# A graph layer with two routed-expert blocks: routing work moved, table lookups shared, the last sums added in place

## The chip, the cores and the metric

One Trainium2 chip, one of its cores. The metric is device microseconds (us) of one execution. Engines in the rows: PE is TensorE's matmul, PEld its weight load, DVE VectorE, ACT ScalarE, POOL GpSimd, SP SyncE, which issues transfers. A letter q behind an engine's name (PEldq, SPq, POOLq) means its sequencer.

## The reference

x has 1250 rows (nodes) of 512 float32, with 40000 edges. Two layers, each a graph part plus a linear-attention mix, and then experts:

```python
xn = layernorm(x)
x = x + L0_gnn(xn, src, dst, ...) + L0_mix(xn[None], ...)[0]
x = x + L0_ffn(layernorm(x)[None], ...)[0]
xn = layernorm(x)
x = x + L1_gnn(xn, edge_index, ...) + L1_mix(xn[None], ...)[0]
x = x + L1_ffn(layernorm(x)[None], ...)[0]

# the experts of either layer, with their own activation:
p = softmax(x @ gate_w)                       # 16 experts
w, idx = top_k(p)                             # 4 in layer 0, 2 in layer 1; weights normalised
y = sum over e of w_e * (act(x @ w1[e] + b1[e]) @ w2[e] + b2[e])    # only for the rows that chose e
y = y + shared experts of every row           # 2 in layer 0 (halved), 1 in layer 1
```

Layer 0 has 256 hidden columns and Gelu. Layer 1 has 384 pairs of gate and up columns with a clamped SwiGLU.

## The kernel before

The program is a row of stages. Each is a block in which every engine has its own instruction list; a stage begins on an engine when all have left the one before. Rows of x stand in ten tiles of 125. The residual is `st.res3`.

**Setup** (L136) loads edges, x in two halves, three small parameter rows, then the mix weights. VectorE works on the edges, waits for the turned parameters (L277, copy L278) and then takes the row moments of x.

**Norm** (`stage_layernorm`, L301): ScalarE's square root (L340), VectorE's reciprocal and scaling, TensorE turns the ten tiles (L334), ScalarE places them (L343). SyncE has nothing here.

**Experts, front** (`stage_front`, L1045). SyncE loads gate, biases, shared weights, b2, writes the normed rows to the DRAM table, and loads the first experts. TensorE makes the logits of three chunks of nodes (500, 500, 250) (L1202) and turns them (L1207). VectorE picks the experts (L1421 to L1452, `mask_ready`) and makes the combine weights (L1468, `comb_ready`). Meanwhile TensorE makes the shared up products in units (one block of hidden columns of one chunk, L1227): 12 units in layer 0, 9 in layer 1. After unit COUNT_AFTER (4 in layer 0, 2 in layer 1) it counts the marks (L1232, L1233, `counted`), and VectorE runs `find_places` (L1325 to L1393), a chain of small instructions that gives each row its slot in a tile of 128 slots and each tile its expert. In layer 1 VectorE's clips and products of the shared SwiGLU (`clip`, `mix`, L1482 to L1494) stand behind `find_places` in its list; ScalarE takes a unit out of PSUM (L1302, L1304) into a ring of four, and TensorE has two pairs of banks for it. After all units TensorE turns the combine weights (L1241), ScalarE places them (L1322), and then the ten shared down tiles follow (L1265, L1267), with `find_rows` (L1251) before the fourth. VectorE adds each to the residual (L1529), and SyncE writes it to the DRAM tensor `token_sums` (L1160).

**Experts, routed** (`stage_routed`, L1906). The number of tiles and each tile's expert are known only on the chip, so the loops are made of registers. There are 48 tiles in layer 0 and 28 in layer 1. For tile g TensorE makes `raise_up(g)` (L2057), then `turn_hidden(g-1)` (L2066), `turn(g+1)` (L2047) and `bring_down(g-1)` (L2075). A matrix product is two passes of an instruction. Before each raise_up and each bring_down its sequencer reads the tile's expert and ring slot from SBUF (`expert_of` L1951, `ring_of` L1954). VectorE adds the bias (L2149) and places the rows (L2142, L2143), ScalarE places the turned hidden rows (L2103), applies Gelu or the sigmoid (L2111, L2108) and weighs the result (L2117).

GpSimd, in one list per tile (L2000): a copy of the row numbers (L1981), the gather of the rows of tile g+4 (L1988), a wait until all adds of earlier experts have landed (L2009), and the add of tile g's result into `token_sums` (L1996). ScalarE's weighing waits for that copy (L2115).

SyncE loads expert e into a ring of three when expert e-3 has been brought down (L962, `load_expert` L992). At the end of layer 0 it reads `token_sums` back; at the end of layer 1 it copies them to the output (L1974) and waits.

## Time and profile before

| | us |
|---|---|
| runs of before, median of 3 (lowest, highest) | 2489.71 (2486.22, 2492.75) |
| the profiled execution, its own time | 2487.18 |
| its span | 2485.1 |
| PE busy | 2205.3 (89%) |
| DVE busy | 1001.1 (40%) |
| ACT busy | 513.2 (21%) |
| POOL busy | 286.9 (12%) |

The profiled execution's own time is 2.1 us over its span and 2.5 us under the median of the runs. A busy TensorE is not one at its peak. What a stage is worth is read from its own stretch of time.

### The profile page before, as it was taken

Reading aid. Unit: us, or ns where it says so; the run is one execution under the profiler, and the core shown is the slowest. Engines: PE = TensorE matmul, PEld = TensorE weight load, DVE = VectorE, ACT = ScalarE, POOL = GpSimd, SP = SyncE. Lnnn points to the kernel's source line nnn. Section 1 sums busy time; section 2 is a strip of 40 time slices with the busy share of each in tenths; the row PEclk is TensorE's granted clock in tenths of the full one; section 3 lists DMA queues with packets and bytes.
Section 4 is the critical chain, followed back from the end, with each engine's and each line's share of the span. In section 5 each row is a group of like instructions: output and inputs, shape, how many; then the busy total and the mean of one; then the engine's idle time right before and its main releaser. Section 6 shows DMA issues by size and latency. Waiting matters only on the chain. (4 is left out here: it accounts for less than half of the span.)

```text
span 2485.1 us, 26904 instructions
## 1 busy us (share of the span) xinstructions
PE 2205.3 (89%) x7344; PEld 1258.0 (51%) x7345; DVE 1001.1 (40%) x2721; ACT 513.2 (21%) x900; POOL 286.9 (12%) x317
## 2 busy tenths in 40 slices
PE   5998979999989988884998899989899898799996
PEld 3444435444454454442543388834488644445553
DVE  7967874302035321222043464311355223634443
ACT  1112221110113022222110254211243112202111
POOL 1200000000000144441200000000000100013332
PEclk9999999999999999997999999989999899899998
DMA  4003000000004267666001000020000103048684
GB/s 119 1 0 112 1 1 17 0 17 0 0 1 135 64 146 167 151 151 151 1 0 59 0 1 1 1 92 0 1 1 1 39 0 127 12 152 274 194 259 115
DMA packets 77265, 159.34 MB, mean 64 GB/s; under 512 B 9133, under 2 KB 20440, under 8 KB 77116
## 3 DMA queue, kind: packets, MB, share of 16 engines
q1 hardware_dynamic: 59516, 115.62, 14.1%
q0 software_dynamic: 17664, 42.64, 8.7%
q8 instruction: 47, 0.77, 0.1%
q14 instruction: 38, 0.31, 0.0%
HBM read 122.06 MB, written 38.74 MB: 65 GB/s over the span
## 5 line engine op out<-in xcount | busy, mean ns | idle before, releaser
L1812 PE MATMUL bank<-arena 125*125 125x257 f32 x1600 | 355.7, 383 | 4.7 <-DVE arena L1731 4.7
L1812 PEld LDWEIGHTS bank<-arena 125*125 125x125 f32 x1600 | 302.2, 189 | 60.4 <-DVE arena L1731 6.3
L2057 PE MATMUL bank<-arena 128*128 x832 | 250.4, 451 | 25.5 <-issue 14.0
L937 PE MATMUL bank<-arena 125*128 125x500 f32 (+1 forms) x720 | 253.0, 512 | 2.3 <-ACT arena L957 2.3
L2057 PEld LDWEIGHTS bank<-arena 128*128 128x128 f32 x832 | 156.6, 194 | 140.8 <-issue 81.4
L1627 PE MATMUL bank<-arena 128*125 128x512 f32 x480 | 211.1, 600 | 8.7 <-DMA arena<-in_L_gnn_W 8.7
L465 PE MATMUL bank<-arena 128*125 128x512 f32 x480 | 213.9, 595 | 2.2 <-PEq L307 1.1
L2075 PE MATMUL bank<-arena 128*128 x360 | 175.3, 616 | 37.7 <-ACT arena L2103 29.8
L937 PEld LDWEIGHTS bank<-arena 125*128 125x128 f32 x720 | 135.6, 189 | 120.0 <-issue 110.1
L2149 DVE TENSOR_TENSOR arena<-bank,arena 128x384 f32<-128x384 f32 (+1 forms) x104 | 51.6, 497 | 307.7 <-PE bank L2057 306.6
L1790 ACT ACTIVATE arena<-arena 125x625 f32<-125x625 f32 x160 | 134.5, 901 | 102.4 <-DVE arena L1731 102.2
L1627 PEld LDWEIGHTS bank<-arena 128*125 128x125 f32 x480 | 90.6, 191 | 122.8 <-issue 113.2
L465 PEld LDWEIGHTS bank<-arena 128*125 128x125 f32 x480 | 87.3, 188 | 102.3 <-issue 101.0
L1731 DVE SCALAR_TENSOR_TENSOR arena<-arena 125x625 f32<-125x625 f32 x160 | 132.4, 864 | 15.9 <-ACT arena L1790 15.9
L1996 POOL DMA_INDIRECT token_sums<-arena x76 | 121.3, 1596 | 147.8 <-DMA token_sums<-arena 97.9
L1663 DVE CUSTOM_DVE_ANT_0 arena<-arena 125x256 f32<-125x256 f32 x160 | 58.5, 421 | 184.9 <-ACT arena L1650 169.2
L756 PE MATMUL bank<-arena 125*125 125x500 bf16 x432 | 112.9, 389 | 19.8 <-DVE arena L731 18.9
L874 DVE TENSOR_TENSOR arena<-bank,arena 128x500 f32<-128x500 f32 (+1 forms) x36 | 21.3, 592 | 264.4 <-PE bank L937 264.4
L731 DVE TENSOR_SCALAR arena<-arena 125x500 bf16<-125x500 f16 x432 | 117.8, 345 | 23.5 <-PE bank L756 22.8
L919 PE MATMUL bank<-arena 128*125 128x512 f32 x240 | 110.1, 622 | 14.6 <-DVE arena L853 9.4
L2075 PEld LDWEIGHTS bank<-arena 128*128 128x128 f32 x360 | 62.3, 189 | 105.2 <-issue 105.2
L1988 POOL DMA_INDIRECT arena<-token_rows,arena x76 | 80.3, 1056 | 171.7 <-DVE arena L2143 143.5
(324 smaller groups left out, 2178.7 us busy)
## 6 DMA issues: line engine op xcount, KB each, us to landing
arena<-in_L_ffn_expert_w SPq DMA_DIRECT2D x16, 1536.0 KB
arena<-in_L_ffn_re_w SPq DMA_DIRECT2D x32, 512.0 KB, 6.4
arena<-in_L_ffn_expert_w SPq DMA_DIRECT2D x16, 768.0 KB, 10.6
arena<-in_L_mix_Wqkv SPq DMA_DIRECT2D x6, 1024.0 KB, 16.4
arena<-in_L_ffn_expert_b SPq DMA_DIRECT2D x16, 384.0 KB
token_rows<-arena SPq DMA_DIRECT2D x2, 2500.0 KB
token_sums<-arena SPq DMA_DIRECT2D x20, 250.0 KB
arena<-in_L_gnn_W SPq DMA_DIRECT2D x1, 4096.0 KB, 12.8
```

The lines of the kernel that those rows point to most:

```text
L465: last = pe.matmul(st.bank[n % 4][0:TS, :], st.turned[:, k, t * TS:(t + 1) * TS], w3[:, k, j * D:(j + 1) * D], start=(k == 0), stop=(k == ...
L731: last = dve.tensor_scalar(marks[:, u, :], st.iota16[:, 0:WIN * NT], float(w * WIN * NT), keys[:, u:u + 1], ALU.add, ALU.is_equal)
L756: last = pe.matmul(bank, stays[:, u, :], marks[:, u, :], start=False, stop=False, skip_group_check=True)
L919: last = pe.matmul(st.bank[s % 4][0:TS, :], X[:, k, s * TS:(s + 1) * TS], w[:, k, :], start=(k == 0), stop=(k == KT - 1))
L937: last = pe.matmul(st.bank[4 + n % 4][:, 0:cn], h[:, s, f * P:(f + 1) * P], st.counts[:, s, c0:c0 + cn], start=(s == 0), stop=(s == NT - 1))
L1627: last = pe.matmul(st.bank[n % 4][0:TS, :], x, w[:, k, half * 512:(half + 1) * 512], start=(k == 0), stop=(k == K - 1))
L1731: dve.scalar_tensor_tensor(out=prob[:, u % 2, s, :], in0=excess[:, n % EXCESS, :], scalar=by_one[:, s, head:head + 1], in1=st.counts16[:, ...
L1790: act.activation(excess[:, n % EXCESS, :], row[:, head, d0:d0 + HALF], ACT.Relu, scale=by_fifth[:, s, head:head + 1], bias=minus_one[:, s, ...
L1812: return pe.matmul(st.bank[n % OUTS][0:TS, 0:ONCOL], prob[:, u % 2, s, j * TS:(j + 1) * TS], st.slots[:, head + 1, s, :], start=(s == 0), ...
L1996: pool.indirect_dma_start(out=sums, out_offset=bass.IndirectOffsetOnAxis(ap=own_row[b][:, 0:1].bitcast(mybir.dt.uint32), axis=0), in_=y[b] ...
L2057: last = pe.matmul(st.bank[UP[b][h]][:, 0:WP], xt[b][:, k, :], rt.ring[:, bass.ds(r, 1), k * W + h * WP:k * W + (h + 1) * WP].rearrange("p ...
L2075: last = pe.matmul(st.bank[DOWN[b]], ht[b][:, f, :], rt.ring[:, bass.ds(r, 1), W2_AT + f * D:W2_AT + (f + 1) * D].rearrange("p a n -> p (a ...
```

## The change

It does eight things.

- Setup: the copy of the turned parameters stands behind the row moments.
- A square root on one throw-away value (`fetch_root`) is put where ScalarE is free: in setup, at the end of the linear stage, and at the end of layer 0's routed stage.
- The gate weights, gate bias, activation scalars and first shared bias are loaded in the norm before the experts, on its SyncE, no longer at the front's start. The other loads of the front keep their order.
- Layer 1 counts behind the first unit, no longer behind the third.
- The combine weights are turned behind the third unit from the end, amid the up products, into banks 6, 7 and 0. Layer 1's down tiles have three banks, no longer four.
- In the routed loop TensorE reads a tile's expert and slot once, between the first and the later products of a bring_down, keeps them in registers, and turns the hidden rows of tile g-1 in the middle of raise_up(g). All lookups for tiles 0 and 1 and the tile count stand before the first raise_up.
- Layer 1's shared result is written to the output itself, and GpSimd adds to it there, with a bound that drops rows past 1249. The copy at the end goes.
- For that the row numbers are one lower.

```diff
@@ stage_setup
-            dve.memset(st.eps, EPS)
+            dve.memset(st.eps, EPS).then_inc(eps_set, 1)
...
-            dve.wait_ge(par_turned, 1)
-            dve.tensor_copy(st.par, st.bank[4][:, 0:3 * LK].rearrange("p (w x) -> p w x", w=3))
             for h, tiles in enumerate(HALVES):
                 dve.wait_ge(x_loaded[h], 32)
                 row_moments(dve, st, range(*tiles), summed)
+            dve.wait_ge(par_turned, 1)
+            dve.tensor_copy(st.par, st.bank[4][:, 0:3 * LK].rearrange("p (w x) -> p w x", w=3))
+        @block.scalar
+        def _(act):
+            act.wait_ge(eps_set, 1)
+            fetch_root(act, st)
@@ new
+def fetch_root(act, st):
+    act.activation(st.any_root, st.eps, ACT.Sqrt)
@@ stage_layernorm
+        if load is not None:
+            block.sync(load)
@@ stage_front
-    COUNT_AFTER = 2 if SW else 4
-    DOWN = [4, 5, 6, 7]
+    COUNT_AFTER = 0 if SW else 4
+    COMBINE_AFTER = NU - 3
+    COMBINE = [6, 7, 0]
+    DOWN = [4, 6, 7] if SW else [4, 5, 6, 7]
...
-            pe.wait_ge(comb_ready, 1)
-            pe.wait_ge(shared_set, 1)
-            pe.wait_ge(up_taken, TAKES * NU)
-            for t in range(NT):
-                c, at = t // 4, (t % 4) * TS
-                last = pe.transpose(st.bank[1 + c][0:total, at:at + TS], comb[:, t, :], st.ident[0:TS, 0:TS])
-            last.then_inc(comb_turned, 1)
+                if m == COMBINE_AFTER:
+                    pe.wait_ge(comb_ready, 1)
+                    pe.wait_ge(shared_set, 1)
+                    pe.wait_ge(counts_used, 1)
+                    for t in range(NT):
+                        c, at = t // 4, (t % 4) * TS
+                        last = pe.transpose(st.bank[COMBINE[c]][0:total, at:at + TS], comb[:, t, :], st.ident[0:TS, 0:TS])
+                    last.then_inc(comb_turned, 1)
...
@@ stage_routed, SyncE and GpSimd
-            else:
-                sp.dma_start(out, sums[1:NODES + 1, :]).then_inc(sums_read[0], 16)
-                sp.wait_ge(sums_read[0], 16)
...
-                    in_=y[b], in_offset=None, compute_op=ALU.add).then_inc(landed[b], 16)
+                    in_=y[b], in_offset=None, compute_op=ALU.add, **bounds).then_inc(landed[b], 16)
@@ stage_routed, TensorE
+                steps = [(h, k) for h in range(PARTS) for k in range(KT)]
+                for n, (h, k) in enumerate(steps):
+                    if n == len(steps) // 2:
+                        between()
...
-            def bring_down(g, b):
-                e, r = expert_of(pe, g), ring_of(pe, g)
+            def bring_down(g, b, r, e, between):
...
+                    if f == 0:
+                        between()
...
-            raise_up(0, 0)
-            more = more_pairs(pe)
-            with pe.Fori(0, more) as i:
-                for b in (1, 0):
-                    g = i * 2 + (2 - b)
-                    raise_up(g, b)
-                    turn_hidden(g - 1, 1 - b)
-                    turn(g + 1, 1 - b, i * 16 + 32)
-                    bring_down(g - 1, 1 - b)
+                first = place_of(0)
+                pe.reg_mov(slot_even, first[1])
+                keep_odd(place_of(1))
+                more = more_pairs(pe)
+                raise_up(0, 0, *first, nothing)
+                with pe.Fori(0, more) as i:
+                    g = i * 2 + 1
+                    odd = kept(expert_odd, NE - 1), kept(slot_odd, R - 1)
+                    raise_up(g, 1, *odd, lambda: turn_hidden(g - 1, 0))
+                    turn(g + 1, 0, i * 16 + 32)
+                    even = []
+                    bring_down(g - 1, 0, kept(slot_even, R - 1), odd[0], lambda: even.extend(place_of(g + 1)))
+                    h = i * 2 + 2
+                    raise_up(h, 0, *even, lambda: turn_hidden(h - 1, 1))
+                    turn(h + 1, 1, i * 16 + 32)
+                    pe.reg_mov(slot_even, even[1])
+                    bring_down(h - 1, 1, odd[1], even[0], lambda: keep_odd(place_of(h + 1)))
```

## Rows read from the trace of the kernel before

**Rows 1.** Busy time by stretch: length, PE, PEld, DVE, ACT, POOL, clock, DMA share, GB/s

```profile
853.00:1140.00 287.00, 227.47 (x864) 138.80 (x864) 56.48 (x144) 69.31 (x144) 136.68 (x148) 0.98 0.65 145
2200.00:2474.00 274.00, 250.44 (x812) 138.37 (x812) 119.95 (x280) 49.88 (x84) 84.19 (x88) 0.97 0.71 208
```

**Rows 2.** Setup's parameter copy (timeline: start, length, engine, line); square root's table loads (ns)

```profile
18.59 0.20 DVE L278 COPY arena<-bank 128x36 f32<-128x36 f32 x1 [2.35 <-PE bank L298]
...
L340 ACT ACT_TABLE_LOAD  x3: 1283/1283/1283, 25.7 to 2061.2; - x3
```

**Rows 3.** TensorE at the start of layer 0's front, layer 1's front, and the mix

```profile
750.81 0.42 PE L1196 MATMUL bank<-arena 16*128 16x16 f32 x4 [2.85 <-DMA arena<-in_L_ffn_gate_w]
...
L1202 PE MATMUL bank<-arena 128*16 128x500 f32 (+1 forms) x24 | 11.5, 647 | 4.8 <-DMA arena<-in_L_ffn_gate_w 4.8
...
1169.97 0.30 PE L448 MATMUL bank<-arena 128*128 128x128 f32 x1 [1.14 <-PEq L307]
```

**Rows 4.** Timeline of layer 0's front, TensorE between up and down products

```profile
798.07 1.23 PE L1241 MATMUL bank<-arena 125*18 125x125 f32 x10 [0.70 <-ACTq L1313]
...
800.89 5.20 PE L1265 MATMUL bank<-arena 128*125 128x512 f32 x8 [1.60 <-ACT arena L1322]
```

**Rows 5.** Timeline of layer 1's front

```profile
2087.46 20.40 PE L1227 MATMUL bank<-arena 128*128 128x500 f32 x48
2094.34 0.25 DVE L1452 TENSOR_SCALAR arena<-arena 125x160 f32<-125x160 f32 x1
2095.74 0.33 DVE L1468 TENSOR_TENSOR arena<-arena 125x160 f32<-125x160 f32 x1
2108.54 0.07 DVE L1336 MEMSET arena<- 125x16 f32 x1 [12.48 <-PE bank L1233]
2132.90 0.54 DVE L1482 TENSOR_SCALAR arena<-arena 128x500 f32<-128x500 f32 x1
2137.70 12.48 PE L1227 MATMUL bank<-arena 128*128 128x250 f32 x48 [9.18 <-ACT arena L1304]
2157.04 5.45 PE L1265 MATMUL bank<-arena 128*125 128x512 f32 x6 [4.63 <-ACT arena L1322]
```

**Rows 6.** Timeline of one tile of layer 1's routed loop

```profile
2240.41 5.32 PE L2057 MATMUL bank<-arena 128*128 x16
...
2245.90 0.60 PE L2047 MATMUL bank<-arena 128*128 128x128 f32 x4
...
2246.84 2.84 PE L2075 MATMUL bank<-arena 128*128 x6 [0.34 <-ACT arena L2103]
...
2249.52 5.36 PE L2057 MATMUL bank<-arena 128*128 x16
...
2249.86 0.62 DVE L2168 SCALAR_TENSOR_TENSOR arena<-arena 128x384 f32<-128x384 f32 x1
```

**Rows 7.** Layer 0's routed loop: timeline of one tile, and the sequencer's loads (ns, minimum/median/maximum)

```profile
1103.82 1.99 PE L2057 MATMUL bank<-arena 128*128 x8 [0.48 <-issue]
...
1106.70 1.98 PE L2075 MATMUL bank<-arena 128*128 x4 [0.23 <-ACT arena L2103]
...
1109.24 1.99 PE L2057 MATMUL bank<-arena 128*128 x8 [0.56 <-issue]
...
L1951 PEldq TENSOR_LOAD <-arena x94: 297/306/1211, 862.6 to 1129.7; - x94
```

**Rows 8.** Layer 0's routed loop: adds of one expert's tiles, and a load of weights

```profile
927.92 1.60 POOL L1996 DMA_INDIRECT token_sums<-arena  x1 [6.19 <-DMA token_sums<-arena]
933.09 0.37 SPq L998 DMA_DIRECT2D arena<-in_L_ffn_re_w  x1
935.74 1.60 POOL L1996 DMA_INDIRECT token_sums<-arena  x1 [0.30 <-issue]
944.12 1.60 POOL L1996 DMA_INDIRECT token_sums<-arena  x1 [4.43 <-DMA token_sums<-arena]
```

**Rows 9.** The line L1974, copy to the output: issue to landing

```profile
DMA to landing us min/median/max: 9.7/9.7/9.7
```

More of the change, by code:

```diff
@@ L1002, in load_expert, with front_inputs, load, stage_experts @@
     sp.dma_start(w2, ins[kind.w2][e].rearrange("(f p) n -> p f n", p=P)).then_inc(rt.w2_loaded, 16)
-def stage_experts(nc, st, ar, kind, ins, kept, out=None, load=None):
+def front_inputs(nc, ar, kind, ins):
+    fi, total = State(), NE + kind.shared
+    fi.brow_w = 2 * P if kind.swiglu else P
+    fi.gw = ar.take(KT * NE).rearrange("p (k e) -> p k e", k=KT)
+    fi.gw_rows = None if kind.gate_b else ar.take(D, NE)
+    fi.gb = ar.take(NE, TS) if kind.gate_b else None
+    fi.act5 = ar.take(total * 5) if kind.swiglu else None
+    fi.b1_rows = ar.take(fi.brow_w, kind.shared * (kind.w1_cols // fi.brow_w))
+    fi.gw_loaded, fi.gb_loaded, fi.act_loaded, fi.b_loaded = (
+        nc.alloc_semaphore(name=f"{what}_loaded_{kind.top}") for what in ("gate", "gate_bias", "act", "first_bias"))
+    def load(sp):
+        if kind.gate_b:
+            sp.dma_start(fi.gw, ins[kind.gate_w].rearrange("(k p) e -> p k e", p=P)).then_inc(fi.gw_loaded, 16)
+            sp.dma_start(fi.act5[:, 0:NE * 5].rearrange("p (o x) -> p o x", o=1),
+                         ins[kind.act].rearrange("e a -> (e a)").unsqueeze(0).unsqueeze(0)
+                         .to_broadcast([P, 1, NE * 5])).then_inc(fi.act_loaded, 16)
+            sp.dma_start(fi.act5[:, NE * 5:],
+                         ins[kind.sact].unsqueeze(0).to_broadcast([P, 5])).then_inc(fi.act_loaded, 16)
+            sp.dma_start(fi.gb, ins[kind.gate_b].unsqueeze(0).to_broadcast([TS, NE])).then_inc(fi.gb_loaded, 16)
+            first_bias = ins[kind.sb1].rearrange("(f n) -> f n", n=fi.brow_w)
+        else:
+            sp.dma_start(fi.gw_rows, ins[kind.gate_w]).then_inc(fi.gw_loaded, 16)
+            first_bias = ins[kind.sb1].rearrange("e (f n) -> (e f) n", n=fi.brow_w)
+        sp.dma_start(fi.b1_rows, first_bias).then_inc(fi.b_loaded, 16)
+    fi.load = load
+    return fi
+def stage_experts(nc, st, ar, kind, ins, kept, fi, out=None, load=None):
     total = NE + kind.shared
@@ L1956, in stage_routed @@
         sums = rt.sums
+        bounds = {} if out is None else dict(bounds_check=NODES - 1, oob_is_err=False)
         @block.sync
@@ L2082, in _, with kept, keep_odd @@
             turn(1, 1, 16)
-            raise_up(0, 0)
-            more = more_pairs(pe)
-            with pe.Fori(0, more) as i:
-                for b in (1, 0):
-                    g = i * 2 + (2 - b)
-                    raise_up(g, b)
-                    turn_hidden(g - 1, 1 - b)
-                    turn(g + 1, 1 - b, i * 16 + 32)
-                    bring_down(g - 1, 1 - b)
-            g = more * 2 + 1
-            raise_up(g, 1)
-            turn_hidden(g - 1, 0)
-            bring_down(g - 1, 0)
-            turn_hidden(g, 1)
-            bring_down(g, 1)
+            with ExitStack() as regs:
+                reg = lambda name: regs.enter_context(pe.register(f"{name}_{kind.top}"))
+                slot_even, expert_odd, slot_odd = reg("slot_even"), reg("expert_odd"), reg("slot_odd")
+                def kept(reg, top):
+                    return nc.s_assert_within(pe.snap(reg), 0, top)
+                def keep_odd(place):
+                    pe.reg_mov(expert_odd, place[0])
+                    pe.reg_mov(slot_odd, place[1])
+                first = place_of(0)
[15 more added lines that the diff above has]
+                    bring_down(h - 1, 1, odd[1], even[0], lambda: keep_odd(place_of(h + 1)))
+                g = more * 2 + 1
+                odd = kept(expert_odd, NE - 1), kept(slot_odd, R - 1)
+                raise_up(g, 1, *odd, lambda: turn_hidden(g - 1, 0))
+                bring_down(g - 1, 0, kept(slot_even, R - 1), odd[0], nothing)
+                turn_hidden(g, 1)
+                bring_down(g, 1, odd[1], odd[0], nothing)
         @block.scalar
@@ L2134, in _ @@
             weigh(g, 1)
+            if out is None:
+                fetch_root(act, st)
         @block.vector
@@ L2212, in build @@
         st.blockmask = held.take(P)
-        st.eps, st.eps6 = held.take(1), held.take(1)
+        st.eps, st.eps6, st.any_root = held.take(1), held.take(1), held.take(1)
         st.inv = held.take(2, TS)
```

79 lines of the change are left out of this document (35 added, 44 removed).

## The prediction

> **What bounds the kernel now.** I first read the busy times by stretch. In both routed loops TensorE is busiest, 227 of 287 us in layer 0 and 250 of 274 us in layer 1, at 0.98 and 0.97 of its clock; GpSimd has 137 us in the first and 84 in the second [rows 1]. So layer 1's loop is TensorE's. Layer 0's is open: TensorE idles 60 us there. Then I read the timelines of the places that the change touches: what TensorE waits for and for how long. A wait counts only where TensorE, or the chain that feeds it, is late; the rest of the span (graph, mix, attention) is untouched, and I cost it at nothing.
>
> **Setup and norms.** VectorE waits 2.35 us for the parameters before the row moments [rows 2]. Moved behind them, the copy still costs its 0.2 us. The parameters are issued behind x on the same queue, so x should have landed by then: 2.15 us gained; bounds 0 (x is what is late) and 2.35. The square root's table is loaded three times, 1.283 us each, on the path of the norm [rows 2]. The new calls put load and root where ScalarE waits for others: 3 x 1.28 = 3.85 us. The Trainium skill ("ScalarE: Activation LUTs", What ACT_TABLE_LOAD costs) adds 1.38 us of drain to each switch, 4.1 us more by its figure; no row here shows a drain, and the sum goes without.
>
> **Gate inputs in the norm.** TensorE waits 2.85 us in layer 0 and 4.8 in layer 1 for the gate weights; a stage begun without a load costs it 1.14 us [rows 3]. The most to gain is 1.7 and 3.7, the least I expect 1.0 and 3.0, if the stage's end costs more here: I take 4.6 for both, near the middle. Loading in the norm costs nothing: SyncE is idle there, and the issues lie beside seven us of scaling and turning. If that cover went, five issues would cost some 2 us.
>
> **Layer 0's front.** Between up and down products TensorE idles 0.70 + 1.60 us, with ten turns of 1.2 us between, and begins the down products slowly: eight passes take 5.20 us [rows 4], where six of the same width take 2.84 at the high clock [rows 6], so eight take 3.7. The turns amid the units cost the same 1.2; the waits and the slow start go: 2.3 + 1.5 = 3.8 us, at least 2.3. The weights are long ready, and the three copies on ScalarE lie beside two units.
>
> **Layer 1's front.** This is the largest part. Today [rows 5]: three units take 20.3 us, so six with the counts end at 2128.5. TensorE then idles 9.18 us until ScalarE has taken unit 4, because the ring waits for VectorE, which is in `find_places` from 2108.54 to 2132.90, 24.4 us. The last three units take 12.48 us in place of 10.2 (half clock at first), the turns and their waits reach to 2157.04, and six down passes take 5.45 us in place of 2.84.
>
> After: the mask is ready at 2094.6, unit 0 ends at 2094.2, so the count waits 0.4 us. `find_places` begins behind the combine weights, 2096.1, and ends at 2120.5. Unit 6 today starts 4.8 us after its end (2137.70 - 2132.90); that is now 2125.3, before TensorE has finished unit 5 at 2128.9. The stall is gone. Three units of 3.4 and 1.1 of turns end at 2140.2, and down begins at 2140.3: 16.7 us earlier, and 2.6 more for the full clock, 19.3. VectorE needs under 24.1 us from the end of `find_places` to its last product (2132.90 to 2157.04, when down began), so it is done by 2144.7, and only the ninth down tile needs the last ones. The fewer down banks cost nothing: VectorE's add is due three tiles later. Lower bound 16, if the ring holds TensorE by one unit.
>
> **Layer 1's routed loop.** A tile takes 9.11 us. The turns begin at 2245.90, four of 0.107 end at 2246.33, down begins at 2246.84: 0.51 us waiting for the placed hidden rows [rows 6]. Turned amid the up products, the rows have 2.6 us of products over them, and the copy is hidden. The hidden values are ready 0.96 us into the next up product (2250.48 against 2249.52), the new turn stands 2.6 in; with the period half a us shorter 0.7 us of slack remains. The lookups within bring_down are issued some 2 us ahead and have a product of 0.86 over them, so they cost nothing. 26 x 0.51 = 13.3 us gained, 0.3 at the end. Lost: all lookups before the first up product, which had two, 2.2 us by the pace of [rows 7]; 0.9 us at tile 0, whose hidden rows arrive after the midpoint of tile 1; and 1 us where the loop catches up with a weight load. Net 9.5; bounds 2 (the slack is not there) and 13.
>
> **Layer 0's routed loop.** A tile of TensorE's work is 8 x 0.214 + 6 x 0.107 + 4 x 0.43 = 4.1 us, yet 5.42 pass. From the first down product to the next up product 2.54 us pass where 1.72 are work: the lookups, two loads of 0.306 us in the median and up to 1.21 at the worst [rows 7]. Hidden placing costs another 0.4. After the change there is one pair of lookups with only 0.86 us of product and 0.44 of lead over it, so about 0.5 us stays inside bring_down: period 4.75 where TensorE binds. By the Trainium skill ("DMA: Bandwidth & Descriptors", Latency and other measured facts) such a load takes about 600 ns at least; the rows show half of that, and by its figure 0.6 us more would stay per tile.
>
> But TensorE seldom binds here. An expert's adds start at 927.92 and 935.74, two of 3.9 us each, and the next expert's first add waits until 944.12 for the last to land, 8.4 us [rows 8]: 16.2 us for three tiles, 5.4 each, whatever TensorE does. The wait is long because the next weights are loaded at 933.09, when the expert has been brought down, just ahead of that add. The lookups inside the down products end them 1.0 us later, and the load with them. I take this as 2 us lost over the ten such experts, between 8 gained and 10 lost. Six tiles at the end and three at the start meet no load; at 4.75 in place of 5.42 they gain 6.0. The lookups ahead of the first up product cost 2.2, and the end gains 0.4. Net 2.2 us gained; bounds -10 and 25.
>
> **The output.** The copy takes 9.7 us from issue to landing [rows 9], after the last add has landed, and the add must land in either kernel: 9.8 us with the wait before it. The bound on the rows is unknown in its price. GpSimd's own work per tile is 3.9 us of 9.1 [rows 6, 8], so it has over 4 us of cover, but the last add has none: 0 to 2 us, I take 0. Writing the ten shared tiles to the output costs what writing them to the scratch tensor does.
>
> **The sum.** 2.15 + 3.85 + 4.6 + 3.8 + 19.3 + 9.5 + 2.2 + 9.8 = 55.2 us. From the execution's own 2487.2 that gives 2432. Against the median of 2489.7 it is 2.3% less. What a measurement of this kernel can tell from no change is about 0.3%, 7.5 us.
>
> **Rivals.** (a) *Layer 0's loop follows TensorE after all.* For it: TensorE idles 60 us in 287. Against it: the adds' chain. All 48 tiles at 4.75 in place of 5.42 gain 32 us, less 2.2 for the lookups at the start: 28 us more than my 2.2, so 2404. (b) *The midpoint turn waits.* VectorE reads registers too; if the hidden rows come after the midpoint, TensorE now stalls with half a product still to do, and what it stood behind before was useful work. For it: only 0.7 us of slack, and a late load in layer 0's lookups. Layer 1's loop then gains 2 in place of 9.5 and layer 0's loses 8: 2432 + 7.5 + 10 = 2449. (c) *The bounded add costs more on GpSimd.* This is the mechanism for slower. GpSimd issues one in 1.6 us and has 8.6 - 3.9 = 4.7 us of room per tile. From 6.3 us per issue it sets the pace of layer 1's 28 tiles, and to eat 55 us an issue must take 1.6 + 4.7 + 2.0 = 8.3 us; at 9 it is 2432 + 28 x 2.7 = 2508. For it: no row shows a bounded one. Against it: the list of rows is the same, and a bound is a comparison. (d) *The front does not gain*, as TensorE waits elsewhere for `find_places`: the turns now wait for `counts_used`. That is ready 5.4 us into it, 2101.5, 30 us before the turns, so I give it nothing.
>
> **How the numbers follow.** Forecast 0.60; (a) 0.13; (b) 0.23, a part of which is its half-way cases; (c) 0.02; the rest 0.02, around no change. The predicted time is the forecast's, 2432. Its own bounds (layer 0's loop -10 to 25, layer 1's 2 to 13, front 16, tables) give 2412 to 2448. Eight times in ten should also take in most of (b) and half of (a): 2406 to 2452. Faster by over 0.3% 0.97, within 0.01, slower 0.02.
>
> **What would show it.** Right: no table load at the norm's root; TensorE's first product 1.1 to 1.8 us after the norm; no idle time of several us in layer 1's up products, down products there at full clock, about 39 us for ten; a tile of layer 1's loop at 8.6 us with no wait for L2103; adds of layer 0's experts still two of 3.9 and one of over 8 us; nothing after the last add. Wrong: TensorE waiting in the middle of an up product (b); layer 0's tiles under 5 us on average (a); GpSimd's add over 1.6 us (c). If the landings grow to 9 or 10 us for every expert, my 2 us for the later loads are too few.

## The result, and the profile after

| us | before | after |
|---|---|---|
| median of the runs (lowest, highest) | 2490.36 of 4 (2486.22, 2492.75) | 2422.99 of 4 (2420.39, 2426.32) |
| the profiled execution, its own time | 2487.18 | 2420.39 |
| its span | 2485.1 | 2417.9 |
| PE busy | 2205.3 (89%) | 2183.7 (90%) |
| POOL busy | 286.9 (12%) | 287.1 (12%) |

After over before is 0.9732, 95% interval 0.9713 to 0.9751: 67.4 us less. The forecast was 2432, 55.2 us less, with 2406 to 2452 as its range. The direction and the likeliest case were right. 12 us more were gained than the sum has, and that is the net of errors of both signs.

The two profiles show where. Each row below takes one instruction that both kernels have and gives its start in both; the difference is what has been gained by then, and the step from row to row is what that stretch gained.

| until the start of | before | after | so far | this stretch | forecast for it |
|---|---|---|---|---|---|
| the first norm's first turn | 28.36 | 24.70 | 3.66 | 3.66 | 3.43 (copy, one table load) |
| layer 0's logits | 751.55 | 746.79 | 4.76 | 1.10 | gate inputs, with layer 1's: 4.6 |
| its first shared up product | 762.99 | 756.53 | 6.46 | 1.70 | 0 |
| its first down tile's bias product | 806.02 | 795.36 | 10.66 | 4.20 | 3.8 |
| its last routed add | 1137.11 | 1119.17 | 17.94 | 7.28 | 2.2 |
| the reciprocal in the last norm | 2062.85 | 2041.50 | 21.35 | 3.41 | 2.57 (two table loads) |
| layer 1's logits | 2074.65 | 2049.87 | 24.78 | 3.43 | in the 4.6 above |
| its first shared up product | 2087.46 | 2059.75 | 27.71 | 2.93 | 0 |
| its first down tile's bias product | 2162.43 | 2114.98 | 47.45 | 19.74 | 19.3 |
| its last routed add | 2468.89 | 2407.07 | 61.82 | 14.37 | 9.5 |
| the end of the span | 2485.1 | 2417.9 | 67.2 | 5.4 | 9.8 |

Four stretches are off by more than 2 us: the logits of both layers (gate inputs: 9.2 for 4.6), layer 0's loop (+5.1), layer 1's loop (+4.9) and the output (-4.4).

The busy time by stretch, columns as in [rows 1], the same two loops:

```profile
842.50:1124.50 282.00, 225.89 (x864) 131.32 (x864) 56.51 (x144) 70.44 (x146) 137.12 (x148) 0.98 0.67 148
2153.00:2412.00 259.00, 242.40 (x812) 136.78 (x812) 120.09 (x280) 47.04 (x84) 83.83 (x88) 0.97 0.70 212
```

TensorE now idles 17 of 259 us in layer 1's loop, 24 of 274 before; in layer 0's it still idles 56 of 282.

**The gate and the logits.** Timeline of TensorE at the start of both fronts, in the kernel after:

```profile
746.79 8.57 PE L1235 MATMUL bank<-arena 128*16 128x500 f32 x24 [0.32 <-DVE arena L1447]
...
2049.87 8.55 PE L1235 MATMUL bank<-arena 128*16 128x500 f32 x24 [1.13 <-PEq L318]
```

and, in the kernel before, the line that answers to the first, with the busy times (columns as in [rows 1]; the clock is the third number from the end) of the first four and a half us of either layer's logits. The prediction used neither:

```profile
751.55 10.26 PE L1202 MATMUL bank<-arena 128*16 128x500 f32 x24 [0.32 <-DVE arena L1410]
```

```profile
751.50:756.00 4.50, 4.45 (x7) 0.91 (x8) 0.00 (x0) 0.00 (x0) 0.00 (x0) 0.64 1.00 330
2074.60:2079.00 4.40, 4.35 (x6) 0.88 (x7) 0.58 (x3) 1.84 (x3) 0.00 (x0) 0.50 0.76 233
```

The waits of 2.85 and 4.81 us [rows 3] are 1.13 now, as forecast. But the 24 passes behind them also went from 10.26 to 8.57 us in layer 0, and from 11.5 [rows 3] to 8.55 in layer 1. Before, they began at a granted clock of 0.64 and 0.50, the lower of TensorE's two levels (1.2 of 2.4 GHz) for part or all of that time; in the kernel after the same stretches have 1.00.

**Layer 1's front**, timeline of TensorE and of two lines of VectorE:

```profile
2059.75 6.98 PE L1260 MATMUL bank<-arena 128*128 128x500 f32 x16
2066.93 0.54 PE L1265 MATMUL bank<-arena 125*125 125x160 f32 x2 [0.21 <-DVE arena L1489]
2067.58 37.07 PE L1260 MATMUL bank<-arena 128*128 128x500 f32 x96
2068.43 0.07 DVE L1373 MEMSET arena<- 125x16 f32 x1
...
2092.80 0.54 DVE L1519 TENSOR_SCALAR arena<-arena 128x500 f32<-128x500 f32 x1
...
2104.49 1.23 PE L1274 MATMUL bank<-arena 125*17 125x125 f32 x10
2105.56 6.92 PE L1260 MATMUL bank<-arena 128*128 128x250 f32 x32
2112.32 2.74 PE L1298 MATMUL bank<-arena 128*125 128x512 f32 x6
```

These answer to [rows 5]. `find_places` begins 8.7 us after the first up product (21.1 before) and takes the same 24.4 us. The 96 passes behind the count run through without a wait, the turns stand amid them, and the six down passes take 2.74 us where they took 5.45.

**Layer 1's loop**, TensorE, from tile 0's hidden rows on; this answers to [rows 6]:

```profile
2170.62 0.52 PE L2109 MATMUL bank<-arena 128*128 128x128 f32 x3 [1.34 <-DVE arena L2236]
...
2176.57 2.74 PE L2099 MATMUL bank<-arena 128*128 x8
2179.15 0.49 PE L2109 MATMUL bank<-arena 128*128 128x128 f32 x3
2179.48 2.75 PE L2099 MATMUL bank<-arena 128*128 x8
2182.06 0.60 PE L2083 MATMUL bank<-arena 128*128 128x128 f32 x4
2182.49 2.74 PE L2119 MATMUL bank<-arena 128*128 x6
```

The reader is to see that only the first line has a wait: tile 0's hidden rows come late, by 1.34 us (0.9 was forecast). From there a tile is 8.50 us (2176.57 here, 2185.07 the next) with nothing in it but products and turns. It was 9.11.

**Layer 0's loop.** GpSimd's adds and SyncE's load at one expert, answering to [rows 8]; then two tiles of TensorE near the end, where no weights are loaded, answering to [rows 7]:

```profile
918.19 1.60 POOL L2032 DMA_INDIRECT token_sums<-arena  x1 [5.38 <-DMA token_sums<-arena]
922.11 1.60 POOL L2032 DMA_INDIRECT token_sums<-arena  x1 [0.30 <-issue]
924.16 0.37 SPq L1011 DMA_DIRECT2D arena<-in_L_ffn_re_w  x1
926.00 1.60 POOL L2032 DMA_INDIRECT token_sums<-arena  x1 [0.30 <-issue]
935.35 1.60 POOL L2032 DMA_INDIRECT token_sums<-arena  x1 [5.64 <-DMA token_sums<-arena]
...
1089.30 1.12 PE L2099 MATMUL bank<-arena 128*128 x4 [0.35 <-issue]
...
1093.95 1.03 PE L2099 MATMUL bank<-arena 128*128 x4
1099.01 1.13 PE L2099 MATMUL bank<-arena 128*128 x4 [0.35 <-issue]
```

TensorE's tiles take 4.65 and 5.06 us (1089.30, 1093.95, 1099.01), 4.86 on average: close to the 4.75 of the forecast. The expert's three adds still take 17.2 us, 3.9 + 3.9 + 9.4: the chain holds, as forecast.

**The end.** The adds of the kernel after, by the tensor that they write, and GpSimd's drain behind the stage in it (ns, minimum/median/maximum; first and last start):

```profile
L2032 POOL DMA_INDIRECT token_sums<-arena x48: 1592/1598/1625, 859.4 to 1119.2; - x48
L2032 POOL DMA_INDIRECT out_x<-arena x28: 1589/1594/1632, 2178.8 to 2407.1; - x28
...
L1971 POOLq DRAIN  x2: 4801/4886/4972, 1124.2 to 2411.5; - x2
```

and the same drain in the kernel before:

```profile
L1933 POOLq DRAIN  x2: 4798/4884/4970, 1142.1 to 2473.7; - x2
```

The bounded add (to out_x) costs GpSimd what the unbounded one costs, 1.59 us. The drain that begins at 2473.7 before, or 2411.5 after, takes 4.8 us. Before, it ran beside the copy of 9.7 us [rows 9]; now nothing covers it.

### The profile page after: what moved, and what is told of

Same layout as the page of the kernel before. It is cut to its first block and busy times, and to the rows that moved or that the text cites. A ratio compares the mean times of both kernels' runs of the same rounds, so it can differ in the third digit from the quotient of the medians.

```text
span 2417.9 us, 26622 instructions
## 1 busy us (share of the span) xinstructions
PE 2183.7 (90%) x7344; PEld 1247.0 (52%) x7345; DVE 1001.3 (41%) x2721; ACT 511.2 (21%) x903; POOL 287.1 (12%) x317
## 5 line engine op out<-in xcount | busy, mean ns | idle before, releaser
L2099 PE MATMUL bank<-arena 128*128 x832 | 257.5, 444 | 16.0 <-issue 8.8
L2099 PEld LDWEIGHTS bank<-arena 128*128 128x128 f32 x832 | 152.0, 192 | 111.2 <-issue 61.3
L2119 PE MATMUL bank<-arena 128*128 x360 | 181.2, 611 | 25.0 <-issue 16.6
L769 PE MATMUL bank<-arena 125*125 125x500 bf16 x432 | 112.6, 389 | 19.9 <-DVE arena L744 18.9
L932 PE MATMUL bank<-arena 128*125 128x512 f32 x240 | 110.0, 621 | 14.6 <-DVE arena L866 9.4
L2119 PEld LDWEIGHTS bank<-arena 128*128 128x128 f32 x360 | 58.6, 189 | 96.0 <-issue 95.7
L769 PEld LDWEIGHTS bank<-arena 125*125 x432 | 57.7, 135 | 74.2 <-issue 64.4
```

What stands on the lines that cost most here:

```text
L769: last = pe.matmul(bank, stays[:, u, :], marks[:, u, :], start=False, stop=False, skip_group_check=True)
L932: last = pe.matmul(st.bank[s % 4][0:TS, :], X[:, k, s * TS:(s + 1) * TS], w[:, k, :], start=(k == 0), stop=(k == KT - 1))
L2099: last = pe.matmul(st.bank[UP[b][h]][:, 0:WP], xt[b][:, k, :], rt.ring[:, bass.ds(r, 1), k * W + h * WP:k * W + (h + 1) * WP].rearrange("p ...
L2119: last = pe.matmul(st.bank[DOWN[b]], ht[b][:, f, :], rt.ring[:, bass.ds(r, 1), W2_AT + f * D:W2_AT + (f + 1) * D].rearrange("p a n -> p (a ...
```

## The experiments

Twelve kernels ran. Each was measured beside the kernel before, whose median was between 2486.6 and 2488.6 us then. Beside the changed kernel it had been 2490.4, so that a difference between one of the totals below and that of the changed kernel can be off by 2 to 4 us for this alone. Where a total moves by less than some 5 us, the reading is from the stretch and not from the total: in six executions that have the changed loop and loads in layer 0, that loop takes 259.7 to 265.4 us from first to last add (mean 262.8), with nothing changed in it. Layer 1's takes 228.3 to 230.6 us in seven executions that have it unchanged. No run undoes the setup or the square roots alone; what they gain is read from the two profiles.

### Layer 0: the weights held back (loads_held)

```diff
                 if e >= R:
-                    sp.wait_ge(down_ready, sp.value_load(
+                    sp.wait_ge(add_begun if out is None else down_ready, sp.value_load(
```

> The changed kernel, with one edit: in layer 0 SyncE loads an expert's weights when the first add of the following expert has begun (its predecessors' adds have then landed), no longer when the old expert's last down product is done. Theory A, the adds are slow to land because the weights are loaded over them: the wait at an expert's boundary, 9.4 us from add to add in the changed kernel, falls to 5.6 (a landing of 4.8 and the issue); three tiles then need 13.4 us of GpSimd against 14.4 of TensorE (4.8 each), where they now take 16.97. Over twelve experts some 31 us less, about 2392 us. Rival B, the last add of an expert lands late for its own reason (it stands behind the gather and two other adds on one queue): the boundary stays over 9 us and the time at 2423, within 3 us. Rival C, the held weights come too late: TensorE waits for them at the start of an expert and the time is over 2423.

Measured: 2407.9 us (2406.44 to 2411.02), ratio 0.9675 (0.9651 to 0.9699), 15 us under the changed kernel, whose interval it doesn't touch. The adds between 875 and 1090 us and, under them, what GpSimd sat idle for ahead of them (us in all, times), in the kernel after:

```profile
L2032 POOL DMA_INDIRECT token_sums<-arena x38: 1597/1599/1602, 878.9 to 1086.5; - x38
...
  DMA token_sums<-arena: 62.8, 14
```

and with the weights held, where the last line is the idle time of those who waited for these adds:

```profile
L2032 POOL DMA_INDIRECT token_sums<-arena x41: 1596/1598/1601, 874.2 to 1086.2; - x41
...
  DMA token_sums<-arena: 24.9, 13
...
  POOL arena L2017: 34.8, 13
```

So 4.5 us of waiting per expert for a landing became 1.9. Theory A holds in kind: the add at an expert's end lands late because the weights come over it. Its size was half of what I expected, 13.5 us in the loop (246.2 from first to last add, 259.7 before the edit) for 31. The last line says why. The weights now come over the following adds, and the copy of row numbers (L2017), which needs the add of two tiles before to have landed, waits 34.8 us in all. An expert takes 16.0 us for 17.0 (12 experts: 874.21 to 1066.15 against 878.89 to 1082.58), not 14.4. Rival B falls, and rival C too.

This edit needs a tile behind each expert that is waited for. With no rows for the last three experts it would wait for ever; it is an experiment, and a version for use would need that case.

### The same on the kernel before (before_loads_held)

> The kernel before, with the same single edit (layer 0's weights held back until the next expert's first add begins). Theory A: its boundary too falls from 8.4 to 10.5 us to 5.6, and then TensorE with its lookups and its late turn of the hidden rows (5.2 to 5.4 us per tile) sets the pace: 3 x 5.3 = 15.9 us for an expert in place of 17.5, some 19 us less, about 2471 us. It would also say that the work taken off TensorE in layer 0 is worth some 12 us more once the weights are held. Rival B: no change, 2490.

Measured: 2476.51 us (2471.78 to 2483.87), ratio 0.9951 (0.9927 to 0.9976): 11 us less for the 19 expected. The adds between 875 and 1100 us, and what GpSimd sat idle for ahead of them:

```profile
L1996 POOL DMA_INDIRECT token_sums<-arena x40: 1591/1597/1600, 877.7 to 1096.3; - x40
...
  ACT arena L2117: 19.2, 18
  DMA token_sums<-arena: 18.3, 14
```

The landings stop being the limit, and the weighed result (L2117), TensorE's product behind it, takes their place in 18 of 40 adds. The loop takes 262.7 us, 16.5 more than with the changed TensorE list. Without held loads the difference between the two lists is 9.3 (269.0 and 259.7). So what TensorE saves in layer 0 seems to be worth more once the adds no longer set the pace. How much more is not shown: these are single profiles of loops that vary by 5.7 us, and by the medians the held loads give 15 us with the changed list and 11 with the old one.

### Hidden rows late, lookups early (hidden_late)

```diff
-                    raise_up(g, 1, *odd, lambda: turn_hidden(g - 1, 0))
+                    raise_up(g, 1, *odd, nothing)
+                    turn_hidden(g - 1, 0)
...
-                    raise_up(h, 0, *even, lambda: turn_hidden(h - 1, 1))
+                    raise_up(h, 0, *even, nothing)
+                    turn_hidden(h - 1, 1)
```

> The changed kernel, with the hidden rows turned after the up products, as before, and the lookups left as changed. Theory: the placing of the hidden rows then lies bare again. In layer 1, 0.51 us on each of 26 tiles, 13 us; the tile goes from 8.50 to 9.0. In layer 0 the adds' chain hides most of it: 0.4 us on the nine or so tiles where TensorE binds, 3 to 4 us. Together 2423 + 17 = 2440. Rival (TensorE binds all through layer 0): 0.4 on 48 tiles, 19 us there, 2455.

Measured: 2467.22 us (2464.74 to 2467.82), 44 us over the changed kernel where I expected 17. A tile of layer 1, timeline of TensorE:

```profile
2268.90 5.32 PE L2099 MATMUL bank<-arena 128*128 x16
2274.06 0.49 PE L2109 MATMUL bank<-arena 128*128 128x128 f32 x3
...
2275.32 1.12 PE L2119 MATMUL bank<-arena 128*128 x2 [0.33 <-ACT arena L2171]
2277.01 1.98 PE L2119 MATMUL bank<-arena 128*128 x4 [0.57 <-issue]
2278.82 5.32 PE L2099 MATMUL bank<-arena 128*128 x16
```

The tile is 9.92 us (2268.90 to 2278.82), worse than the 9.11 of before. There are two gaps. The one of 0.33 I expected. The other, 0.57 behind the first down product, is the lookups. They stand behind that product in the list; its wait for the placed rows also holds the sequencer, and so the two register loads start when the engine does, with 0.86 us of product over 1.4 us of sequencer. From the first to the last add layer 1's loop takes 263.1 us for 228.3, and layer 0's 273.6 for 259.7.

### Lookups as before, hidden rows amid (lookups_each)

```diff
-                    bring_down(g - 1, 0, kept(slot_even, R - 1), odd[0], lambda: even.extend(place_of(g + 1)))
...
+                    raise_up(g, b, *place_of(g), lambda: turn_hidden(g - 1, 1 - b))
+                    turn(g + 1, 1 - b, i * 16 + 32)
+                    e, r = place_of(g - 1)
+                    bring_down(g - 1, 1 - b, r, e, nothing)
```

> The changed kernel, with the lookups made as before, a pair ahead of every raise_up and every bring_down, and the hidden rows still turned in the middle. Theory: in layer 1 a tile was 9.13 us, of which 0.51 was the placing, so 0.12 is the lookups', 3 us over 26 tiles, of which 1 comes back as the first up product starts earlier. In layer 0 some 0.4 us where TensorE binds, 4 us, of which 2 come back at the start. Together 2423 + 4 = 2427. Rival: the lookups cost TensorE half a us on all 48 tiles of layer 0, 24 us, about 2447.

Measured: 2429.12 us (2427.01 to 2431.26), 6 us over the changed kernel; 4 were expected, 24 by the rival. Layer 1's first up product starts 2.1 us earlier (107.75 us after its logits, for 109.86) and its loop takes 2.3 more (230.6 for 228.3), as much as that loop varies by itself. Layer 0's takes 5.5 more (265.3), at the upper end of its scatter. The intervals of the two ratios (0.9737 to 0.9784, and 0.9713 to 0.9751) overlap, so the 6 us are not clear of noise.

### Both undone (loop_as_before)

> The changed kernel with TensorE's routed loop exactly as before: late turns and a pair of lookups ahead of every raise_up and bring_down. lookups_each alone cost 6 us and hidden_late alone 44 us. Theory: the two undone edits do not add up to 50 us. With the lookups behind the first down product, that product's wait for the placed rows also holds TensorE's sequencer, so the lookups of 1.4 us lie bare; ahead of bring_down they lie beside up products. So this kernel is faster than hidden_late: layer 1's tile 9.1 us again, against 9.9; its loop, first to last add, 245 us against 263; layer 0's about 269; the whole 2423 + 17 + 7 = 2447. Rival (each edit has its own price): 2470 or more.

Measured: 2442.97 us (2441.09 to 2446.56), 24 us under hidden_late. One tile of layer 1:

```profile
2248.76 5.39 PE L2099 MATMUL bank<-arena 128*128 x16
...
2255.30 2.84 PE L2119 MATMUL bank<-arena 128*128 x6 [0.39 <-ACT arena L2153]
2257.97 4.36 PE L2099 MATMUL bank<-arena 128*128 x13
```

It takes 9.21 us (2248.76 to 2257.97); the loops take 246.6 and 271.7 us. So undoing the turn alone costs 44 us, undoing the lookups alone 6, and undoing both 20. The new place of the lookups is at best a gain of 6 us with the turn in the middle; under a late turn it is a loss of 24 us. The rival (each edit has its own price) falls.

### The gate inputs (gate_in_front, gate_in_front_busy)

```diff
         @block.sync
         def _(sp):
+            fi.load(sp)
             s1 = [ins[kind.sw1]] if SW else [ins[kind.sw1][n] for n in range(kind.shared)]
```

with no load in the norm, and for the second kernel also:

```diff
         def _(pe):
+            for n in range(9 if SW else 4):
+                pe.matmul(st.bank[5][:, 0:500], st.ident, st.turned[:, n % KT, 0:500], start=True, stop=True)
             pe.wait_ge(gw_loaded, 16)
```

> The changed kernel, with the gate inputs loaded at the start of the front again. Theory: both the wait and the half clock behind it come back. Layer 0: 1.7 us of wait, and logits in 10.3 us in place of 8.6; layer 1: 3.7 us of wait, and 11.5 us in place of 8.6. Together 10.0 us more than the changed kernel, 2433. Rival (the prediction's sum, waits alone): 5.4 us more, 2428.

> As gate_in_front, with products into a bank that nobody reads (4 in layer 0, 9 in layer 1, 0.42 us each) made by TensorE while it waits for the gate weights. Theory: the half clock comes from TensorE's idle time of 2.9 and 4.8 us ahead of the logits, so with that time filled the logits run in 8.6 us in both layers, and only the waits stay: 5.4 us over the changed kernel, 4.6 us under gate_in_front. Rival: the half clock has another cause (the logits' own shape, or a moment at which the chip lowers it anyway): as slow as gate_in_front.

Measured: 2435.45 us (2429.04 to 2438.94) and 2436.94 us (2436.28 to 2441.47). The busy times of the first 4.5 us of both layers' logits (the clock is the third number from the end), in gate_in_front and then in gate_in_front_busy:

```profile
750.80:755.30 4.50, 4.46 (x7) 0.85 (x8) 0.00 (x0) 0.00 (x0) 0.00 (x0) 0.65 1.02 340
2062.10:2066.60 4.50, 4.41 (x7) 0.91 (x8) 0.57 (x3) 1.84 (x3) 0.00 (x0) 0.62 0.59 86
```

```profile
748.30:752.80 4.50, 4.50 (x11) 1.07 (x12) 0.00 (x0) 0.57 (x1) 0.00 (x0) 1.00 0.96 322
2062.10:2066.60 4.50, 4.50 (x12) 1.07 (x12) 0.00 (x0) 0.57 (x1) 0.00 (x0) 1.00 0.96 371
```

The lowered clock is there with the wait (0.65, 0.62) and gone when the wait is filled (1.00, 1.00).

From the first logit product to the first shared up product gate_in_front takes 11.43 and 11.59 us, gate_in_front_busy 9.74 and 9.90, the changed kernel 9.74 and 9.88. The products without a reader take away 1.7 us of slowness in each layer, so the slow start comes from TensorE's idle time ahead and not from the logits. The rival falls by these stretches. The total does not show it, since I had mis-sized the filling. A product is two passes of 0.43 us, so nine take 7.8 us and not 3.8, and they overran the wait: from the norm's last turn to the logits gate_in_front_busy takes 8.8 us in layer 1, where gate_in_front takes 4.2, and 5.4 for 3.6 in layer 0. Of gate_in_front's total, 12 us over the changed kernel, 8.3 us are seen to be the edit's: the two waits (1.8 and 3.1) and the two slow starts (1.7 and 1.7). Its profiled execution is even 17.5 us longer; the other 9 us lie in stretches that the edit does not touch, over 4 of them in the routed loops. Layer 1's wait was 4.21 here, not 4.81, and the slow start 1.7, not 2.9. The profiles of before_loads_held and before_out_sums, which have the front of before, also take 11.59 us there and not the 12.81 of the table: the same loss comes in another size from run to run, and 2.9 is the largest of it.

### Layer 1's front (count_late, combine_last)

```diff
-    COUNT_AFTER = 0 if SW else 4
+    COUNT_AFTER = 2 if SW else 4
```

> The changed kernel, with layer 1's count behind its third unit, as before. Theory: find_places starts 12.5 us later, TensorE again waits some 9 us for the ring of four units behind it, and falls to half its clock there for 2 us more; the turns of the combine weights, amid the units, move with them. Layer 1 from logits to the routed loop's first up product takes 110 + 12 = 122 us; the whole 2435. Rival (the gain came from the combine weights turned amid the units): under 4 us more.

Measured: 2438.05 us (2432.93 to 2442.22), 15 us more. The old stall is back (TensorE's timeline):

```profile
2116.94 6.35 PE L1260 MATMUL bank<-arena 128*128 128x250 f32 x16 [9.17 <-ACT arena L1345]
```

From logits to the routed loop's first up product it takes 121.60 us for 109.86: 11.7 us, as expected (12).

combine_last turns the combine weights behind the last unit in both layers, and ScalarE places them behind its last sigmoid.

> The changed kernel, with the combine weights turned behind the last unit again in both layers (banks as changed). Theory: layer 0 loses the 4.2 us that it gained (two waits and the slow start of the down products); layer 1 loses the wait for the turned weights, 1.5 us, and the slow start, up to 2.6: 3 to 4 us. Together some 8 us more, 2431. Rival: with the stall in layer 1 gone the ring still has units to take there, so that turning them late costs nothing in layer 1: 4 us more in all.

Measured: 2434.43 us (2432.81 to 2437.29), 11 us more. In layer 0, from the first shared up product to the routed loop's, 94.02 us for 92.42: 1.6 us, not 4.2. In layer 1, logits to first up product, 117.75 for 109.86: 7.9 us, not 3 to 4. TensorE's timeline in layer 1:

```profile
2113.98 1.23 PE L1274 MATMUL bank<-arena 125*17 125x125 f32 x10
2121.01 4.17 PE L1298 MATMUL bank<-arena 128*125 128x512 f32 x5 [5.79 <-ACT arena L1329]
```

TensorE waits 5.79 us for ScalarE, whose placing stands behind sigmoids that wait for VectorE. Amid the units it stands ahead of them. The two parts of layer 1's front are worth 11.7 and 7.9 us, 19.6 together, and the stretch gained 19.74.

### The output and the drain (before_out_sums, drain_early)

before_out_sums has the output part of the diff alone: sums in the output, bounded adds, row numbers one lower, no copy.

> The kernel before, with the output part alone: layer 1's sums are kept in the output, the adds are bounded, the copy goes. Theory: from the start of the last add to the end of the span the kernel before takes 16.2 us and the changed kernel 10.8, since GpSimd's drain at the end of the stage, 4.8 us, lay beside the copy and now lies bare; so 5.4 us less, 2483 against 2488. Rival (the prediction's sum): 9.8 us less, 2478.

Measured: 2481.81 us (2473.4 to 2485.1, 10 runs), ratio 0.997 (0.9956 to 0.9985): 6 us less. The total alone does not exclude 9.8. The profile does: from the last add's start (2470.9) to the end of the span (2481.7) it is 10.8 us, 16.2 in the kernel before, and the drain lies in it:

```profile
L1934 POOLq DRAIN  x2: 4801/4886/4972, 1145.1 to 2475.3; - x2
```

drain_early moves the last wait off GpSimd:

```diff
+            if out is not None:
+                landings, gathers = [sp.value_load(rt.all_landed[0:1, n:n + 1], min_val=32, max_val=16 * TILES + 32)
+                                     for n in range(2)]
+                for b in range(2):
+                    sp.wait_ge(landed[b], landings)
+                    sp.wait_ge(rows_loaded[b], gathers)
```

> The changed kernel, with the wait for the last adds and gathers of layer 1 on SyncE and no longer on GpSimd, so that GpSimd's drain begins as soon as its last add is issued (three small VectorE instructions in layer 1's find_places make the two numbers that SyncE waits for). Theory A: the drain is GpSimd's own 4.8 us, whatever is in flight: from the last add's start to the end of the span 1.4 + 4.8 + 1.6 = 7.8 us in place of 10.8, 3 us less, 2420. Rival B: the drain waits for the transfer that the last add started and then takes its 4.8 us: no change.

```profile
L1977 POOLq DRAIN  x2: 4972/5987/7002, 1126.5 to 2411.0; - x2
```

The last drain begins at 2411.0, 0.2 us ahead of the last add's start (2411.2), and ends at 2418.0. The add landed at 2415.6, when SyncE's wait ended, so the drain ended 2.4 us after the landing and not 4.8. From the last add to the end of the span it is 8.4 us for 10.8. Theory A, with 2.4 us for the 3 expected. The total, 2423.47 (2420.51 to 2433.52), does not show it.

### Three edits together (best)

```diff
-                keep_odd(place_of(1))
-                more = more_pairs(pe)
-                raise_up(0, 0, *first, nothing)
+                raise_up(0, 0, *first, lambda: keep_odd(place_of(1)))
+                more = more_pairs(pe)
```

with the edits of loads_held and drain_early.

> Three edits on the changed kernel: the held loads of layer 0 (15 us less as measured), the drain of drain_early (0 to 3), and the lookups of tile 1 and of the tile count in the middle and behind the first up product, in either layer. Five register loads stand ahead of the first up product now, of which two remain; a pair with its checks takes the sequencer 1.4 us, so 2 us less in each layer. Together 18 to 22 us less than the changed kernel: 2401 to 2405. If the sequencer is then late at the first tile's hidden rows, the 4 us are not there: 2405 to 2408.

Measured: 2403.2 us (2401.64 to 2407.92, 5 runs), ratio 0.9665 (0.9643 to 0.9687), against 0.9732 (0.9713 to 0.9751) of the change: some 20 us faster than the changed kernel. Against loads_held alone it is 4.7 us, with intervals that overlap. The lookups gave 1.6 us in layer 0 (first shared up product to first add, 101.28 for 102.91). In layer 1 the first up product starts 2.1 us earlier and the loop takes 2.2 more (230.5 for 228.3). One us of this is lost at tile 0, which runs at a lower clock. Busy times from the start of tile 0's up products to tile 1's, in the kernel after and in combine_last, which has the same loop in layer 1:

```profile
2159.72:2166.53 6.81, 6.81 (x17) 3.94 (x17) 0.56 (x1) 0.00 (x0) 0.00 (x0) 0.77 0.85 278
2170.37:2178.32 7.95, 7.95 (x16) 4.47 (x17) 0.56 (x1) 0.00 (x0) 0.00 (x0) 0.66 0.88 311
```

The same stretch takes 7.77 us in best and 7.81 in the kernel before, both at 0.67. In the seven executions with layer 1's loop unchanged, tile 0 took 6.7 to 6.8 us in three and 7.8 to 8.1 in four. So neither best nor lookups_each (7.9 us) settles what the lookups' place is worth in layer 1.

## Why the prediction was right, and where its sum was off

**Setup, norms.** Right: 3.66 us in the first stretch for 3.43; no row of the kernel after has a table load at the norm's root, and the same three loads, 1.28 us each, now stand where ScalarE was waiting anyway. The 4.1 us more of the Trainium skill's figure ("ScalarE: Activation LUTs", What ACT_TABLE_LOAD costs) are not there. The last norm gained 1.29 us at its root, one load and no drain. Nor is there one where ScalarE had just worked: in the kernel before, an activation at 2076.38 us (0.23 long) is followed by a load at 2076.62 (1.28) and the next activation at 2077.92.

**Gate inputs.** "4.6 for both" was half. The waits were sized rightly, down to the 1.13 us that stay. The step that failed is that the sum priced only the wait. What it left out is the slow start behind it: the logits' 24 passes are 1.7 and 2.9 us shorter. The prediction had used this very effect for the down products of both fronts, and had [rows 3] with 647 ns a pass before it. gate_in_front and gate_in_front_busy show the cause. The 2.9 is the larger of the two sizes that layer 1's slow start has in the profiles; with the other, 1.7, the sum for both layers would be off by 3.4 us and not 4.6.

**Layer 0's front.** 4.2 for 3.8. That all of it comes from the turns' place is not shown: combine_last gives back 1.6 only, 1.8 over the stretch of the table. There the eight first down passes took 3.67 us behind the same 1.60 us of wait that goes with 5.20 before [rows 4], so the slow start was not of that wait alone: before, TensorE had idled 0.70 us more, ahead of the turns. combine_last keeps the other half of the edit, the banks: the turns into 6, 7 and 0 need not wait until ScalarE has taken the last unit out of 1 to 3, and the 0.70 us is gone there. With it went the 1.5 us of the slow start, 2.2 of the 2.4 us that combine_last still gains in that stretch. That the one brought the other is likely; no run changes the banks alone.

**Layer 1's front.** 19.7 for 19.3, and both mechanisms stood: `find_places` 12.4 us earlier takes away the stall of 9.2 us (count_late, 11.7 us), and the turns amid the units take away ScalarE's lateness (combine_last, 7.9). The second is more of a wait than I had said: the placing was queued behind sigmoids.

**Layer 1's loop.** 14.4 for 9.5. "26 x 0.51" took the placing alone; the tile went from 9.11 to 8.50, so 0.61, with 0.1 for the lookups between the products, which I had costed at nothing. That is 2.6 us. The lookups at the start cost 2.1 (2.2 forecast), tile 0's hidden rows 1.3 (0.9), and the weights 1.9 in two stalls (0.99 and 0.90), but the kernel before had one of 1.6 itself, so that only 0.3 of my 1 us was a loss. The last tile gained 1.0, not 0.3. Another 1.0 us was luck: tile 0 took 6.80 us for 7.81 at a higher granted clock (0.77 for 0.67, see best), as in three of seven executions with this loop. From the first down tile's bias product to the last add these seven take 294.0 us on average, and three with the loop of before 307.2, so that 13 us is a fairer figure than 14.4. "They cost nothing" held for the lookups within bring_down, but for a reason that I gave only in part ("issued some 2 us ahead"): the lead is there because the turn in the middle leaves no wait right ahead of the down products. hidden_late shows what they cost without it, 0.8 us a tile more than before. Rival (b), the midpoint turn waits, has one stall within this loop, at tile 0: the slack, forecast at 0.7 us, was mostly 0.5 to 0.7.

**Layer 0's loop.** 7.3 for 2.2 in this pair of profiles. The picture was right: TensorE at 4.86 us where it binds, the adds at 3.9 + 3.9 + 9.4, later loads of weights and longer landings (9.4 for 8.4). The step that failed is "16.2 us for three tiles": it was one expert's [rows 8]. The boundaries before step by 16.2, 18.5, 16.2, 18.9, 16.7 and 18.3 us from 927.92 on, 17.5 on average over twelve (one of them has four tiles and one two); in every second expert the third add had waited for TensorE. After, each expert of three tiles takes 16.4 to 17.5, and the twelve 17.0 on average. So twelve experts gained 6.3 us where I had put a loss of 2, and the first and last tiles gained 3 where I had put 6. Part of this is the pair of profiles: over the same stretch as in the table, the two profiles with the loop of before take 331.1 and 333.3 us and the six with the changed loop 323.8 to 329.3, 327.0 on average. So some 5 us is what can be said, with single pairs from 2 to 9.

**The output.** 5.4 for 9.8. "Nothing after the last add" was wrong. The copy went, but GpSimd's drain, 4.8 us, had lain beside it. The prediction asks what is late next when a wait goes; here it did not ask. The profile of before shows the drain at 2473.7, at the copy's own start.

**The bound on the rows** costs nothing: 1.594 us an add, 1.598 without. Rival (c) falls. Rival (a), layer 0's loop follows TensorE, did not come about: three adds still take 17 us, and TensorE's own tiles would take 14.6.

**The bounds.** "2412 to 2448" does not follow from the list beside it: layer 0's loop alone, at 25 us for 2.2, would give 2409.

## What to carry to other kernels

When a wait of an engine goes, price the clock that it cost as well: read the mean duration of the first passes behind it against the same shape elsewhere. When the last transfer of a kernel goes, look at what ran beside it, each engine's closing drain too. And two edits of one engine's list are not a sum: a lookup is free only where the sequencer runs ahead, and one semaphore wait just before it takes that lead away.

## What the runs showed of the hardware that I had not expected

GpSimd's drain at the end of both routed stages takes 4.8 to 5.0 us although its last indirect transfer has landed when it begins, and, begun with the last add, ends 6.8 us after that add's start. At the ends of other blocks of the kernel after it takes from 0.03 to 11.1 us; what sets its length is not shown. By the Trainium skill ("Perfetto Trace Analysis", DMA Instruction — SWDGE (GPSIMD)) the end shown for such an instruction is when the last descriptor is written, and the processor finishes later. That can be a part of it; no run here separates it, and the drain takes 4.8 us also when it starts 4.4 us behind the add.

An add into the DRAM sums lands late when 1 MB of weights is loaded over it. In the kernel before, layer 0's adds take 4.9 us to land in the median and 8.0 at most. The wait for it at an expert's end is 4.5 us on average with the load and 1.9 us when the load begins behind it (the changed kernel and loads_held).
